# Expert logits as four 128-column products with tokens on 128 partitions, and level weights in three instructions

## What is computed

```python
def reference(...):                       # cut to what matters
    xn = _layernorm(x)
    x = x + _L0_attn_ref(xn, ...) + _L0_ffn_ref(xn, ...)
    xn = _layernorm(x)
    return x + _L1_attn_ref(xn, ...) + _L1_ffn_ref(xn, ...)

def _L0_ffn_ref(...):                     # 8 experts of width 32, top 1
    logits = xt @ Wg.T
    top1 = jnp.argmax(logits, axis=-1)
    ...                                   # xhat: second layer norm of xt
    def body(y, p):
        h = gelu((xhat * s_e + b_e) @ w1 + bb1)
        out = h @ w2 + bb2
        return (y + (top1 == eid)[:, None] * out, None)

def _L1_attn_ref(...):                    # 16 heads, hierarchical levels
    Lam = softplus(Lp * dl)               # one weight per token, head and level
    ...                                   # cg: running sum of the gates g
    decay = exp(where(tri, cg_t - cg_s, -1e30))
    lam_ts = Lam[t, h, level(t, s)]       # level: size class of t XOR s
    Y = (scores * decay * lam_ts) @ V
    ...                                   # output product, skip, layer norm
```

## Time and profile before

| | before |
|---|---|
| time, median of 3 runs | 1116.2 us (1115.88 to 1116.23) |
| profiled execution | 1117.61 us, of it span 1116.1 us |
| mean granted TensorE clock | 0.992 |
| busy in the span: PE, DVE, ACT, POOL | 1061.7, 933.6, 696.0, 249.0 us |
| DMA, mean over the span | 25 GB/s |

### The profile page before, as it was taken

The page is one execution under the profiler, slowest core; times in us unless marked ns, Lnnn a source line. Parts: engine busy times, 40 slices in busy tenths (PEclk is TensorE's granted clock), DMA queues, the critical chain, the costliest instruction groups (busy, mean ns, idle before and its releaser), DMA issues. The chain is left out here.

```text
span 1116.1 us, 18645 instructions
## 1 busy us (share of the span) xinstructions
PE 1061.7 (95%) x5980; PEld 668.1 (60%) x5980; DVE 933.6 (84%) x2077; ACT 696.0 (62%) x1509; POOL 249.0 (22%) x235
## 2 busy tenths in 40 slices
PE   6999999999999999999999999999999999999995
PEld 3665657566565665657566565665657566565663
DVE  6797896979889797897979889797997979889677
ACT  4593846738386592846738385582846749285582
POOL 0040310313122031310303121031311303131086
PEclk9999999999999999999999999999999999999998
DMA  3000000000000000000000000000000000000435
GB/s 145 19 2 10 1 19 10 0 28 0 19 9 19 9 0 28 0 19 9 0 28 0 19 9 19 9 0 28 0 19 9 0 28 0 19 9 19 170 94 161
DMA packets 31907, 27.61 MB, mean 25 GB/s; under 512 B 1552, under 2 KB 25744, under 8 KB 31760
## 3 DMA queue, kind: packets, MB, share of 16 engines
q1 hardware_dynamic: 31888, 27.37, 7.5%
HBM read 15.57 MB, written 11.80 MB: 25 GB/s over the span
## 5 line engine op out<-in xcount | busy, mean ns | idle before, releaser
L1752 POOL TENSOR_TENSOR pair<-pair,cgt 128x512 f32<-128x512 f32 x64 | 94.7, 1508 | 525.3 <-DVE pair L1515 525.3
L984 ACT ACTIVATE gx<-p 128x512 f32<-128x512 f32 x256 | 147.2, 596 | 27.7 <-PE p L538 21.3
L536 PE MATMUL p<-x1Th,Gl 128*128 128x512 f32 x256 | 120.4, 470 | 0.3 <-ACT gx L984 0.3
L939 ACT ACTIVATE gelu<-p,bias_u 128x512 f32<-128x512 f32 x32 | 22.0, 687 | 157.8 <-PE p L483 157.8
L538 PE MATMUL p<-x1Th,Gh 128*128 128x512 f32 x256 | 101.2, 395 | 0.0
L537 PE MATMUL p<-x1Tl,Gh 128*128 128x512 f32 x256 | 101.0, 395 | 0.0
L647 PEld LDWEIGHTS p<-vbd,pair 128*128 128x128 f32 x512 | 62.0, 191 | 41.2 <-issue 26.8
L1782 POOL TENSOR_TENSOR skip<-skip,W 128x512 f32<-128x512 f32 x15 | 19.2, 1277 | 295.0 <-DVE skip L1296 295.0
L610 PE MATMUL p<-gx,x1T 128*32 128x512 f32 x512 | 68.2, 604 | 12.0 <-DVE pair L1526 11.2
L622 PE MATMUL p<-nodesT,K 128*128 128x512 f32 x128 | 66.7, 603 | 12.7 <-DVE nodesT L1488 12.7
L647 PE MATMUL p<-vbd,pair 128*128 128x128 f32 x512 | 74.0, 288 | 0.0
(11 more groups left out here) (267 smaller groups left out, 2701.6 us busy)
## 6 DMA issues: line engine op xcount, KB each, us to landing
xin<-in_x SPq DMA_DIRECT2D x16, 256.0 KB, 2.8
hx_scratch<-vdw SPq DMA_DIRECT2D x15, 256.0 KB, 2.6
res_scratch<-res SPq DMA_DIRECT2D x14, 256.0 KB, 2.0
gx<-in_weights SPq DMA_DIRECT2D x1, 1216.0 KB, 10.1
vp<-hx_scratch SPq DMA_DIRECT2D x4, 256.0 KB, 3.4
GT<-res_scratch SPq DMA_DIRECT2D x4, 256.0 KB, 3.3
out<-vp SPq DMA_DIRECT2D x4, 256.0 KB, 3.2
W<-in_weights SPq DMA_DIRECT2D x1, 746.0 KB, 11.1
```

Of the source, the lines that this page charges most:

```text
L536: pe.matmul(head_bank(h)[:, :], tile(Gl, h), x1Th[:, :], start=True, stop=False)
L984: act.activation(tile(gx, h, T), head_bank(h)[:, :], ACT.Copy).then_inc(R["gx_copied"], 1)
L1752: pool.tensor_tensor(pw, pw, spread(cgt[:, H * n:H * n + H].unsqueeze(2), [128, H, CHUNK]), ALU.subtract)\
```

## The change

Logits: four products, each 32 columns of `WgT` with one tile of 128 tokens, into rows 32c to 32c + 31 of the bank, 128 columns wide. `turn_logits`, `top1`, `oh_b` and `mask_b` then work on 128 partitions and 128 columns (of the three-fold one-hot, 24 rows of each 32). The number of instructions of top1 stays. `gate_u` runs its `W1` product first, then waits for the mask, and adds four bf16 products of 128 columns, one per tile; `expert_b` and `b2_b` have four blocks of columns, each with the values in the 32 rows of its tile and zeros elsewhere. `out0` takes all 128 rows. In the set-up, TensorE spreads the expert and bias constants over the 128 rows with eight more products, VectorE copies them out of PSUM and multiplies them by `own_chunk`; `rank` is made by eight memsets. Level weights become three instructions: two multiply `lam`, the mask (a column each) and `e4` in one go for two levels of 64 columns, the third does the two other levels without a mask. In `last()`, VectorE waits for `c_ready` ahead of `node_lams`.

The diff without its context lines:

```diff
--- before.py
+++ after.py
@@ -115,8 +115,9 @@
-        expert_b = sb("expert_b", E * HID, bf16, 32)
-        b2_b = sb("b2_b", D, bf16, 32)
+        expert_b = sb("expert_b", 4 * E * HID, bf16)
+        b2_b = sb("b2_b", 4 * D, bf16)
+        rank = sb("rank", E)
@@ -134,13 +135,12 @@
-        lgT = sb("lgT", T, fp32, 32)
-        oh = sb("oh", T, fp32, 32)
+        lgT = sb("lgT", 128)
+        oh = sb("oh", 128)
-        am = lv[0:32, :]
-        mask_b = sb("mask_b", T, bf16, 32)
-        oh_b = sb("oh_b", T, bf16, 32)
+        mask_b = sb("mask_b", 128, bf16)
+        oh_b = sb("oh_b", 128, bf16)
@@ -342,6 +342,12 @@
+                pe.wait_ge(R["consts_loaded"], 16)
+                rows, at, width = k("ident", 0, 32, 32), cat["expert"][0], E * HID + 3
+                for c in range(4):
+                    to = slice(32 * c, 32 * c + 32)
+                    pe.matmul(P1[0][to, 2:2 + width], rows, K[0:32, at:at + width], start=True, stop=True)
+                    mm = pe.matmul(P1[0][to, 2 + width:2 + width + D], rows, w("b2", rows=32), start=True, stop=True)
             def inner_products():
@@ -441,7 +447,9 @@
-                pe.matmul(P0[2][0:32, :], w("WgT"), xnT[:, :], start=True, stop=True).then_inc(R["logit_ps"], 1)
+                for c in range(4):
+                    mm = pe.matmul(P0[2][32 * c:32 * c + 32, 0:128], w("WgT"), tile(xnT, c), start=True, stop=True)
+                mm.then_inc(R["logit_ps"], 1)
             def deltas(j):
@@ -471,17 +479,17 @@
             def gate_u(j, q):
-                pe.wait_ge(R["top1_steps"], 7 * j + 7)
-
-                pe.matmul(P0[q][:, :], expert_b[0:8, 128 * q:128 * q + 128], mask_b[0:8, :],
-                          start=True, stop=False)
-                pe.matmul(P0[q][:, :], w("W1", 128 * q, 128 * q + 128), xhT[:, :],
-                          start=False, stop=True).then_inc(R[f"u{q}_ps"], 1)
+                pe.matmul(P0[q][:, :], w("W1", 128 * q, 128 * q + 128), xhT[:, :], start=True, stop=False)
+                pe.wait_ge(R["top1_steps"], 7 * j + 7)
+                for c in range(4):
+                    at = E * HID * c + 128 * q
+                    mm = pe.matmul(tile(P0[q], c), expert_b[:, at:at + 128], mask_b[:, :], start=False, stop=(c == 3))
+                mm.then_inc(R[f"u{q}_ps"], 1)
             def out0(j):
@@ -493,7 +501,7 @@
-                    mm = pe.matmul(o, oh_b[0:24, t], b2_b[0:24, :], start=False, stop=True)
+                    mm = pe.matmul(o, oh_b[:, :], tile(b2_b, n), start=False, stop=True)
@@ -997,7 +1005,7 @@
-                    act.wait_ge(R["alpha_steps"], 2 * i)
+                    act.wait_ge(R["alpha_steps"], i)
@@ -1193,26 +1201,30 @@
-                step(dve.tensor_copy(expert_b[:, :], k("expert", rows=32)))
+                step(dve.tensor_copy(th[:, 512:512 + E * HID + 3 + D], P1[0][:, 2:2 + E * HID + 3 + D]))
+                step(dve.tensor_tensor(view(expert_b[:, :], "p (c x) -> p c x", c=4),
+                                       spread(th[:, 512:512 + E * HID].unsqueeze(1), [128, 4, E * HID]),
+                                       spread(k("own_chunk").unsqueeze(2), [128, 4, E * HID]), ALU.mult))
             def expert_sums():
-                b2 = w("b2", rows=32)
-                part, rest = th[0:32, 0:128], th[0:32, 128:256]
-                step(dve.memset(th[0:32, 256:384], 0.0))
+                at = 512 + E * HID
+                b2_part, b2 = th[:, at:at + 3], th[:, at + 3:at + 3 + D]
+                first_part, part, rest, total = b2_b[:, 0:128], th[:, 0:128], th[:, 128:256], th[:, 256:384]
+                step(dve.memset(total, 0.0))
-                    step(dve.tensor_copy(b2_b[:, :], b2 if n == 0 else rest))
-                    step(dve.tensor_copy(part, b2_b[:, :]))
+                    step(dve.tensor_copy(first_part, b2 if n == 0 else rest))
+                    step(dve.tensor_copy(part, first_part))
-                    step(dve.scalar_tensor_tensor(th[0:32, 256:384], part, k("b2_part", n, n + 1, 32), th[0:32, 256:384],
-                                                  ALU.mult, ALU.add))
-                step(dve.tensor_copy(b2_b[:, :], th[0:32, 256:384]))
+                    step(dve.scalar_tensor_tensor(total, part, b2_part[:, n:n + 1], total, ALU.mult, ALU.add))
+                step(dve.tensor_tensor(view(b2_b[:, :], "p (c d) -> p c d", c=4), spread(total.unsqueeze(1), [128, 4, D]),
+                                       spread(k("own_chunk").unsqueeze(2), [128, 4, D]), ALU.mult))
             def later_weights():
@@ -1260,6 +1272,8 @@
+                for e in range(E):
+                    dve.memset(rank[:, e:e + 1], float(E - e))
@@ -1322,27 +1336,27 @@
             def turn_logits(j):
-                dve.transpose(lgT[:, :], P0[2][0:32, :]).then_inc(R["top1_steps"], 1)
+                dve.transpose(lgT[:, :], P0[2][:, 0:128]).then_inc(R["top1_steps"], 1)
             def top1(j):
-                eq = view(am[:, 0:128], "p (c e) -> p c e", e=E)
-                val = view(am[:, 128:256], "p (c e) -> p c e", e=E)
-                mx, mx2 = am[:, 512:528], am[:, 528:544]
+                eq = view(lv[:, 0:32], "p (c e) -> p c e", e=E)
+                val = view(lv[:, 32:64], "p (c e) -> p c e", e=E)
+                mx, mx2 = lv[:, 512:516], lv[:, 516:520]
-                dve.tensor_tensor(eq, lg, spread(mx.unsqueeze(2), [32, 16, E]), ALU.is_ge).then_inc(R["top1_steps"], 1)
+                dve.tensor_tensor(eq, lg, spread(mx.unsqueeze(2), [128, 4, E]), ALU.is_ge).then_inc(R["top1_steps"], 1)
-                dve.tensor_tensor(val, eq, spread(k("rank", rows=32).unsqueeze(1), [32, 16, E]), ALU.mult)\
+                dve.tensor_tensor(val, eq, spread(rank[:, :].unsqueeze(1), [128, 4, E]), ALU.mult)\
-                rows = view(oh[:, :], "p (c r e) -> p c r e", c=16, e=E)
+                rows = view(oh[:, :], "p (c r e) -> p c r e", c=4, e=E)
-                    last = dve.tensor_tensor(rows[:, :, r], val, spread(mx2.unsqueeze(2), [32, 16, E]), ALU.is_equal)
+                    last = dve.tensor_tensor(rows[:, :, r], val, spread(mx2.unsqueeze(2), [128, 4, E]), ALU.is_equal)
@@ -1495,17 +1509,15 @@
             def level_weights(i):
+                l = view(lam[:, :], "p (m l) -> p l m", l=LEVELS)
-                for n in range(TILES):
-                    last = dve.tensor_tensor(view(alpha[:, :], "p (l k h) -> p l k h", l=4, k=TILES)[:, :, n],
-                                             view(lam[:, :], "p (k h l) -> p k l h", k=TILES, l=LEVELS)[:, n, 6:10],
-                                             spread(view(k("alpha_mask"), "p (l k) -> p l k", l=4)[:, :, n:n + 1], [128, 4, H]),
-                                             ALU.mult)
-                last.then_inc(R["alpha_steps"], 1)
-                dve.wait_ge(R["alpha_steps"], 2 * i + 1)
-                dve.tensor_tensor(alpha[:, 0:64], alpha[:, 0:64], e4[:, 0:64], ALU.mult)
-                dve.tensor_tensor(alpha[:, 64:256], alpha[:, 64:256], e4[:, 128:320], ALU.mult).then_inc(R["alpha_steps"], 1)
+                for n, at in enumerate((0, 128)):
+                    dve.scalar_tensor_tensor(tile(alpha, n, 64), e4[:, at:at + 64], k("alpha_mask", TILES * n, TILES * n + 1),
+                                             l[:, 6 + n], ALU.mult, ALU.mult)
+                dve.tensor_tensor(view(alpha[:, 128:256], "p (l m) -> p l m", l=2),
+                                  view(e4[:, 192:320], "p (l m) -> p l m", l=2), l[:, 8:10], ALU.mult)\
+                    .then_inc(R["alpha_steps"], 1)
             def token_rows(i):
@@ -1701,6 +1713,7 @@
+                dve.wait_ge(R["c_ready"], B)
```

## The result

The changed kernel takes 1076.9 us (median of 4 runs, 1076.83 to 1077.35) against 1116.2 us of the kernel before (4 runs, 1115.88 to 1117.15). The ratio is 0.965, with a 95% interval of 0.964 to 0.966. The forecast was 1098 (1091 to 1107): the direction was right, and the gain is twice what I had summed, 39.3 us and not 18.3. The profiled execution of the changed kernel has a span of 1075.7 us, against 1116.1.

The account below looks back on a forecast made before the run. TensorE was taken as the bound, busy in 65.02 of a pass's 66.80 us. Logits and mask products (-6.9), the pair weights' wait (-10.5) and set-up (-0.9) made -18.3 us: 1098 us, range 1091 to 1107.

Parts of the forecast that it names:

- Logits: Four 32-column products side by side on TensorE take 0.36 us in place of 0.98: -0.62 us in each of 15 passes.
- Rival 3: The logits' four products do not run side by side and take 0.98 us as before: 1107 us; chance 0.07.
- Mask products: In gate_u, four bf16 products with four weight loads in place of one: +0.08 us each, +0.16 us a pass.
- rival 4: The four mask products run one after the other, 1.28 us in place of 0.32, slower than before: 1124 us; chance 0.05.
- W1 first costs and gives nothing: In gate_u, the W1 product ahead of the wait for top1 changes nothing, since top1 is already over: 0 us.
- The pair weights' wait: TensorE's 0.75 us wait for L1526 at the third pair_scores goes whole in 14 passes: -10.5 us.
- rival 1: The pair weights' wait stays whole (1108 us) or half (1103 us); chance 0.17.
- the thin margin: At the third pair_scores, VectorE has only 0.2 us to spare for the pair weights' wait to go whole.
- The nodes' wait: TensorE's 0.77 us wait for the transposed nodes turns into one for ScalarE's copies (L1055), worth nothing.
- Rival 2: The nodes' wait is worth its time if ScalarE's chain shortens or starts sooner: 15 x 0.75 us more, 1087; chance 0.07.
- Top1 and level weights on VectorE: In the loop, top1 goes from 3.36 to 1.9 us and level weights from 3.92 to 2.0 us.
- Set-up: Ahead of the loop: -0.9 us (bounds -2.0 and +1.0), with VectorE at its first scan input about 0.9 us sooner.

Follow-up runs that it names:

- b_out128: Kernel before, with only out0's bf16 bias product reading 128 rows (the added rows zero) in place of 24: 1101.5 us.
- b_rows64_96r: Kernel before, with out0's bias product on 64 rows and the mask product on 96, second run, at a clock of 0.995: 1109.9 us.
- b_w1first: Kernel before, with gate_u's W1 product moved ahead of the 8-row mask product: 1113.2 us.
- b_newlw: Kernel before, with the three-instruction level weights alone and the last pass's wait for c_ready: 1105.5 us.
- a_oldlw: Changed kernel, with the six-instruction level weights of before put back: 1077.7 us.
- a_act_late: Changed kernel, with ScalarE's pair_distance and pair_decay of tiles 2 and 3 moved behind node_matrices: 1061.5 us.
- a_late_oldlw: a_act_late with the six-instruction level weights of before put back: 1073.4 us.
- b_rows128: Kernel before, with both out0's bias product and gate_u's mask product on 128 rows, the added rows zero: 1096.4 us.
- b_out24_fp32: Kernel before, with out0's 24-row bias product on float32 operands, so out0 never changes type: 1131.8 us (one run).
- a_best: a_act_late with norm2 of the sample before moved from ahead of level_sum(i, 0) to behind pair_weights(i, 2): 1059.2 us.

## Why the prediction was off

*The bound.* Right: TensorE was the bound and is it still, busy in 62.94 of 64.27 us.

*Logits.* Right to the hundredth, from L655's rows of the same form. Rival 3 is out.

*Mask products: the step that failed, with out0.* I saw 0.10 us more around each bf16 product than its columns need, and put it down to "changes to and from fp32". So it stayed in the sum for gate_u, and for out0 I wrote 0 since the columns and the load don't change. What it is: a stop of TensorE when the rows of a product change between 64 or fewer and 128. It was to be had in both places. I had costed the edit's price (loads) and never asked what about the old product was special, though a row of 24 of 128 rows between four of 128 showed a difference in two things, type and rows. The earlier trace rows had more to say than the load's length of 0.09 us, the only thing I took from it: the load starts with its product, while that of the gelu product ahead starts 0.11 us before its own (502.93 and 503.04). The Trainium skill, page "TensorEngine Tiling (Array Packing)", section "Tiling Modes" (its key properties), states that a change of tiling mode drains TensorE; it lists 32, 64 and 128 rows as modes. The trace agrees, with 0.10 us going in at 8, 24, 32 and 64 rows and with the 96-row product counting as 128. The page gives no figure. By it alone, with the 0.10 us of the rows, out0 would have been an estimated -0.8 us a pass, and the forecast some 12 us lower.

In size, over fifteen passes: out0 -0.98 for 0, 15 us; gate_u -0.58 for +0.16, 11 us. These 26 us are more than the 21 that the forecast lacked. The wait below (3.5 us) and 0.18 us a pass around norm1's transposes (2.7 us), which come with out0's edit alone (b_out128) and whose cause I can't place, take 6 back, and the set-up, below, gives 1.4 more than its term. The term for the four loads was wrong too, by little: four products of 128 columns with four weights hold TensorE 0.23 us (34.01 to 34.24 in the changed kernel's set-up, where a product of their own shape follows; in the loop it is 0.32 with the 0.10 that chunk_sums' shape costs), as one of 512 columns does (0.22, 560.05 to 560.27 in b_rows64_96r). Neither a cost per load nor rival 4's waits exist here. "W1 first costs and gives nothing" holds in the changed kernel with its 128 rows; with narrow mask products it would have been worth 0.2 us (b_w1first).

*The pair weights' wait.* Mechanism right (b_newlw), size off: -0.50, not -0.75, 3.5 us over 14 passes. The prediction had TensorE at the third pair_scores 0.23 us behind VectorE. gate_u(0) lies ahead of it, and came out 0.30 shorter and not 0.08 longer, 0.38 us sooner; that leaves a wait of 0.15, and 0.25 was measured. So rival 1 held for a third of the wait, but not by its mechanism: the thin margin was noted, and looked at from VectorE's side only. TensorE's faster arrival used it up. Where I gave the saving to nodes and top1 together, either alone does it (b_newlw, a_oldlw).

*The nodes' wait.* Right: worth nothing, by the chain of ScalarE's copies, which starts from TensorE's heads; 0.82 us before L604 instead. Rival 2 named its own condition, "if ScalarE's chain gets shorter", and a_act_late with a_late_oldlw shows that condition to hold: 15.4 us.

*Top1 and level weights on VectorE.* Top1 took 528.26 to 530.3, 2.0 us (predicted 1.9). Level weights:

```profile
513.18 1.60 DVE L1516 SCALAR_TENSOR_TENSOR alpha<-e,K,lam 128x64 f32<-128x64 f32 x2
514.70 0.82 DVE L1518 TENSOR_TENSOR alpha<-e,lam 128x128 f32<-128x128 f32 x1
515.45 0.86 DVE L1299 BATCH_NORM_STATS2 st<-skip 128x6 f32<-128x128 f32 x4
```

2.27 us (513.18 to 515.45), predicted 2.0; GpSimd's products run beside them as before.

*Set-up.* -2.25 and not -0.9, but these 2.25 us can't be set beside the term, since TensorE's clock differs between the two traces in three places. VectorE comes to the first scan input at 25.27 us, 24.67 in before: 0.6 later, where I had 0.9 sooner. In both it waits there for TensorE (0.89 and 1.38 us), and TensorE had run at half speed for part of the way, in the changed kernel in one product and in before in another. L459 and L367 are L451 and L361 of before:

```profile
15.40 1.99 PE L451 MATMUL p<-xnT,W 128*128 128x512 f32 x4
...
20.33 3.39 PE L361 MATMUL p<-y,gx 128*128 128x256 f32 x8
```

```profile
17.39 3.78 PE L459 MATMUL p<-xnT,W 128*128 128x512 f32 x4
...
22.33 1.99 PE L367 MATMUL p<-y,gx 128*128 128x256 f32 x8
```

b_w1first has the set-up of before except for the order in gate_u, and a_oldlw that of the changed kernel; in both traces these products are short (1.98 and 1.99 us) and the first values products long, so they can be compared. From the start of the logits VectorE comes to the first scan input after 13.26 us in b_w1first (10.22 to 23.48) and after 14.19 in a_oldlw (9.63 to 23.82): 0.9 later, where I had 0.9 sooner; in a_act_late, with the same set-up, it is 13.70, 0.4 later. VectorE doesn't wait there in any of the three. But ahead of it, what top1 saves is lost again: in a_oldlw VectorE waits 2.19 us for ScalarE's sp (L923), in b_w1first 0.40, and so it comes to the bias 1.0 us sooner (7.70 against 8.66 behind the logits' start) and not 1.8. Then come expert_b's 1.22 us and b2_b's longer instructions. The sum had a slip as well: 1024 columns at 1.01 ns are 1.03 us and not the 1.2 that I wrote. But the first heads start after 39.38 us in b_w1first and after 38.28 in a_oldlw, 1.1 sooner. So the term comes out near its -0.9, but by luck: VectorE's part has the wrong sign, and what makes up for it, beside out0's stops, was not followed.

## What to carry to other kernels

Look at the partition count of every matmul that stands between full ones: here a product on 64 rows or fewer cost TensorE two stops, 0.25 to 0.3 us together, and zeros up to 96 or 128 rows removed them for nothing but a memset. The row of its weight load tells them: it starts with the product, and not ahead of it. Where it can't be widened, put it beside a product whose shape differs anyway. When a row takes longer than its work, list everything in which it differs from its neighbours and cost the edit by each, before one reason is taken. And price a wait together with the wait that ends just behind it: here one edit was worth 10.6, 0.8 and 11.9 us on three kernels that do the same work.

## What the runs showed of the hardware

The stop of TensorE at a change of rows: 0.10 us before the narrow product (0.32 against 0.22), 0.10 behind it (0.16 against 0.06), and 0.05 (out0) to 0.1 us (gate_u) more in the product after that; 8, 24, 32 and 64 rows show it, 96 and 128 don't. Going in it is the same for bf16 and fp32. It costs nearly as much in out0 for one product of 128 columns (0.25 us) as in gate_u for one of 512 (0.30). Weight loads on 128 or 96 rows start 0.11 us ahead of their product, those on 64 or fewer with it. That the exposed load is what costs the 0.10 us, and not something that holds back load and product together, is not shown.

A change of the columns written does the same: W1's or xnT's product of 512 columns takes 0.86 us ahead of a product of its own shape (539.14 to 540.00) and 0.95 ahead of chunk_sums (553.47 to 554.42, before), and chunk_sums' loads start with it.

The clock in the set-up. The first values products (eight of 432 columns) take 4.86 us in before and 3.17 in the changed kernel:

```profile
46.71 4.86 PE L521 MATMUL p<-W,x1T 128*128 128x432 f32 x8 [0.69 <-ACT x1T L957]
```

```profile
46.15 3.17 PE L529 MATMUL p<-W,x1T 128*128 128x432 f32 x8 [0.69 <-ACT x1T L965]
```

From 40 to 50 us the granted clock was 0.85 in before and 1.00 in the changed kernel, a mean over the two levels, 1.2 and 2.4 GHz. TensorE was busy in 8.50 of these 10 us in both, and in 9.13 of the 10 ahead of them, at 1.00, in both. Of the thirteen profiled executions that ran at full clock in the passes, five have the short form (b_out128, b_rows128, b_rows64_96r, b_out24_fp32 and the changed kernel), and the others, a_best and a_act_late among them, the long one. b_out24_fp32 and b_w1first differ in this, though in both all products from 15 to 40 us ran at full clock. The executions of one kernel differ in their clock too: the fastest of before (1114.2 us) had 0.995 on average, the slowest (1118.6) 0.992.

The changed kernel paid for it earlier. Its products from 15.37 to 21.10 (L357 and the first two of L459; rows of 2.09 and 3.78 us) have rows of 1.14 and 1.98 or 1.99 us in each of the other twelve. The granted clock reads 1.00 for that stretch of its trace, as it does for the logits of before that took 1.92 us at 10.55: at the start of a span the reading can't be relied on, and the length of a known product can. a_oldlw, without that slow stretch but with the long values products, has its first heads at 47.91, 0.9 us sooner than the changed kernel. So the clock worked both ways in the set-ups, and no share of the 39.3 us can be given to it; the length of a pass, at 1.00 in before and in the changed kernel, is free of it. What decides the clock stays open.
